# Attention with undivided probabilities, and the last batch's feed-forward spread over a recurrence's first steps

## The reference, cut to what matters

```python
# layer 0, x: (8, 256, 512)
xn = rms_norm(x, g_norm) * (1 + scale) + shift          # scale, shift from cond @ W_emb
q, k, v = heads(xn @ W_qkv)                             # 16 heads of 32
attn = softmax(rms_norm(q, g_q) @ rms_norm(k, g_k).T * 32 ** -0.5)
o = attn @ v;  x1 = o + o @ W_out
w_up, w_down = dequant4bit(...)                         # plus low-rank terms
x = x + relu(x1 @ w_up + ... + b_up) @ w_down + ... + b_down    # hidden 2048
# layer 1: a recurrence over all 256 positions
for t in range(256):                                    # q, p: (8, 512)
    q, p = rk4(q, p, drive=x[:, t])                     # four times tanh(q) @ coupling.T
    y[:, t] = q
x = x + shared_expert(y) + top2_of_8_experts(y)
```

## Time and profile before

| what | value |
| --- | --- |
| median of three runs | 3059.54 us (3057.57 to 3059.79) |
| profiled execution | 3062.81 us, of which the instructions span 3061.1 us |
| PE busy in the span | 2788.1 us (91%) |
| DVE, ACT, POOL busy | 1827.7, 1121.8, 1354.7 us |
| mean granted clock of PE | 0.921 |
| layer 0, to the barrier | 0 to 993.6 us of the span |
| the recurrence's first group, 32 steps | 1003.7 to 1219.8 us |
| the later groups, to the end | 1219.8 to 3061.1 us |

### The profile page before, as it was taken

The page is one execution under the profiler, slowest core; times in us unless marked ns, Lnnn a source line. Parts: engine busy times, 40 slices in busy tenths (PEclk is TensorE's granted clock), DMA queues, the critical chain, the costliest instruction groups (busy, mean ns, idle before and its releaser), DMA issues.

```text
span 3061.1 us, 132271 instructions
## 1 busy us (share of the span) xinstructions
PE 2788.1 (91%) x48208; PEld 2427.2 (79%) x48208; DVE 1827.7 (60%) x6585; ACT 1121.8 (37%) x4950; POOL 1354.7 (44%) x3466
## 2 busy tenths in 40 slices
PE   6778989889888556999999999999999999999998
PEld 4346667667767455999999899899899899899987
DVE  2657656755764444666666666666666666566654
ACT  1224433644552223333333333333333333333321
POOL 1220000111110666666666566566566566666600
PEclk7569999999999555999999999999999999999999
DMA  4523222533441000344444444444444344344466
GB/s 142 171 80 107 82 86 58 176 125 114 141 147 32 25 0 0 112 126 131 131 130 129 123 129 131 125 129 128 124 130 128 121 131 130 109 145 127 132 217 198
DMA packets 137163, 359.87 MB, mean 118 GB/s; under 512 B 15888, under 2 KB 24720, under 8 KB 136592
## 3 DMA queue, kind: packets, MB, share of 16 engines
q1 hardware_dynamic: 136336, 354.17, 37.8%
q10 hardware_dynamic: 672, 3.67, 0.3%
HBM read 323.31 MB, written 34.47 MB: 117 GB/s over the span
## 4 chain that ended last, share of the span: by engine, by line
PE 61%; DVE 2%; issue 2%; ACT 1%; DVEq 0%; DMA 0%; POOL 0%; POOLq 0%; SPq 0%
PE pscan L1234 13%; PE pscan L1230 13%; PE pg L1161 11%; PE pd L1187 11%; PE pu L1161 11%; ACT th L1088 1%; DVE state L1350 1%; DVE carry L1350 0%; PE prouter L1245 0%; DMA wd<-w_split 0%; PE prouter L1253 0%; PE pd L1260 0%; DVE pscan L1336 0%; DVEq L1349 0%; DVE th L1333 0%
## 5 line engine op out<-in xcount | busy, mean ns | idle before, releaser
L1230 PEld LDWEIGHTS pscan<-th,carry 128*128 128x128 f16 x16384 | 555.7, 97 | 135.6 <-ACT th L1088 114.9
L1230 PE MATMUL pscan<-th,carry 128*128 128x8 f16 x16384 | 564.4, 167 | 100.6 <-ACT th L1088 100.4
L1234 PE MATMUL pscan<-th,carry 128*128 128x16 f16 x16384 | 561.9, 170 | 3.0 <-DVE th L1333 2.3
L1234 PEld LDWEIGHTS pscan<-th,carry 128*128 128x128 f16 x16384 | 486.8, 97 | 4.5 <-DVE th L1333 4.5
L1088 ACT ACTIVATE th<-state 128x32 f16<-128x32 f32 x768 | 176.1, 229 | 733.0 <-DVE state L1350 733.0
L1161 PE MATMUL pg<-qh,wgu 128*128 128x256 f16 x3168 | 430.1, 275 | 14.5 <-issue 14.5
L1187 PE MATMUL pd<-hg,wd 128*128 128x256 f16 x3168 | 428.9, 274 | 2.8 <-DMA wd<-w_split 2.8
L1161 PE MATMUL pu<-qh,wgu 128*128 128x256 f16 x3168 | 429.2, 275 | 1.9 <-issue 1.8
L1350 DVE TENSOR_REDUCE state<-pscan 128x32 f32<-128x96 f32 x768 | 197.1, 257 | 268.0 <-PE pscan L1234 262.8
L1161 PEld LDWEIGHTS pg<-qh,wgu 128*128 128x128 f16 x3168 | 295.5, 98 | 53.3 <-issue 15.9
L1161 PEld LDWEIGHTS pu<-qh,wgu 128*128 128x128 f16 x3168 | 295.0, 98 | 37.1 <-issue 2.6
(11 more groups left out here) (203 smaller groups left out, 4573.3 us busy)
## 6 DMA issues: line engine op xcount, KB each, us to landing
wgu<-w_split SPq DMA_DIRECT2D x264, 512.0 KB, 3.6
wd<-w_split SPq DMA_DIRECT2D x264, 384.0 KB, 3.1
parts_mem<-in_w_tiles SPq DMA_DIRECT2D x120, 256.0 KB, 3.0
w_split<-parts_mem SPq DMA_DIRECT2D x99, 256.0 KB, 2.2
late<-in_w_tiles SPq DMA_DIRECT2D x78, 256.0 KB, 3.2
w_split<-late SPq DMA_DIRECT2D x33, 128.0 KB, 3.0
out<-oo SPq DMA_DIRECT2D x8, 512.0 KB, 4.0
xs<-in_x SPq DMA_DIRECT2D x1, 3584.0 KB, 13.2
```

Of the source, the lines that this page charges most:

```text
L1230: mm(pscan[:, 0, m * B:(m + 1) * B], clo[:, k, m * P:(m + 1) * P], th[:, k, 0, :], start=(m == 0 and k == 0), stop=False, skip_group_check ...
L1234: ins = mm(pscan[:, 0:2, m * B:(m + 1) * B], chi[:, k, m * P:(m + 1) * P], th[:, k], start=False, stop=(k == NC - 1), skip_group_check=True)
```

## The change

- **Probabilities stay undivided.** `normed` goes. PE transposes a head as soon as ACT has its exponential (`a_exp`). DVE takes the reciprocals of four heads at once (`inverse`), ahead of the quad's last copy. Ahead of each quad's `weighted`, PE writes the reciprocals, spread over 32 partitions each, into the free half of the same bank: eight fp32 matmuls of 128 columns with a broadcast column of `rinv` as weights and the identity as moving data. ACT copies these to `oT` (`widened`), and DVE multiplies the product by them (`gathered`).
- **The next batch's input moves forward.** ACT squares it after the first quad (was the third), PE's `norm_sum` stands in the second quad behind head 5 (was the fourth), ACT's `norm` after the second quad, DVE's `normed_input` after the third quad (was between the last two copies). PE writes these sums into the other bank's half.
- **Batch 0's pieces.** ACT converts piece 4c+4 after head 4c+2, and pieces 4c+5 to 4c+7 after head 4c+3.
- **The last batch's feed-forward is cut in two.** In layer 0 only columns 0 to 31 are made: 192 up-matmuls of 32 columns into two banks, ReLU and split in halves, 192 down-matmuls, one addition. Columns 32 to 255 are made inside the recurrence's first 32 steps: `fill` issues five matmuls of 224 columns behind each stage's `chi` product in stages 0 to 38 (up) and 41 to 79 (down), with ACT's and DVE's parts a few stages behind and POOL waiting for the result in step 31.
- **The coupling's maximum moves forward.** DVE takes it between batch 7's last `gathered` and its sums, POOL reduces it before batch 7's largest value, and `chi` is made between `scale` and `low` of batch 7.
- **The first 32 steps are written out** on all four engines: `walk`'s first loop is now one of Python. `w_up`, `w_dn`, `hid`, `late`, `fs` and `bsc` live through both layers, `w_qkv` only in layer 0, and `kp` moves from `carry` to `fs`.

```diff
+                if b == B - 1:
+                    pl.wait_ge(S["mx"], 1)
+                    pl.partition_all_reduce(kp[:, 1:2], kp[:, 0:1], P, bass.bass_isa.ReduceOp.max).then_inc(S["par"], 1)
...
-            pl.partition_all_reduce(kp[:, 1:2], kp[:, 0:1], P, bass.bass_isa.ReduceOp.max).then_inc(S["par"], 1)
...
-                    if not ffn and 3 <= h and h + 1 < PIECES:
-                        weights_high(h + 1)
                     highs(NC + h)
-                def gathered(c):
+                def pieces(h, count):
+                    for piece in range(h + NC, min(h + NC + count, PIECES)):
+                        if not ffn:
+                            weights_high(piece)
+                def widened(c):
                     act.wait_ge(S["p_pv"], b * NC + c + 1)
-                    if c == 2 and b + 1 < B:
-                        act.wait_ge(S["p_nrm"], b + 2)
-                    act.activation(oT[:, c, :], Ob[c % 2][:, 0:T], ACT.Copy).then_inc(S["a_oT"], 1)
+                    act.activation(oT[:, c, :], Ob[c % 2][:, T:2 * T], ACT.Copy).then_inc(S["a_wide"], 1)
                 for c in range(NC):
                     exps(HPC * c)
                     exps(HPC * c + 1)
                     if c:
-                        gathered(c - 1)
-                    if c == NC - 1 and b + 1 < B:
-                        norm(b + 1)
+                        widened(c - 1)
                     relus(ffn_quad[c][0:2])
                     exps(HPC * c + 2)
+                    pieces(HPC * c, 1)
                     relus(ffn_quad[c][2:3])
                     exps(HPC * c + 3)
+                    pieces(HPC * c + 1, HPC - 1)
                     relus(ffn_quad[c][3:])
-                    if c == NC - 2 and b + 1 < B:
+                    if c == 0 and b + 1 < B:
                         if b == 0:
                             act.wait_ge(S["xs_in"], 16)
                         squares(b + 1)
-                gathered(NC - 1)
+                    if c == 1 and b + 1 < B:
+                        norm(b + 1)
+                widened(NC - 1)
...
-            for j in range(RELUS):
-                relu(B - 1, j)
+            for half in range(2):
+                act.wait_ge(S["p_up"], (B - 1) * RELUS + half + 1)
+                bank = first_up[half][:, 0:RELUS * G]
+                for m in range(RELUS):
+                    part = bank[:, m * G:(m + 1) * G]
+                    ins = act.activation(part, part, ACT.Relu, bias=bsc[:, half * RELUS + m:half * RELUS + m + 1])
...
+                act.activation(hid[:, half * RELUS:(half + 1) * RELUS, 0, 0:G], bank.rearrange("p (a t) -> p a t", t=G), ACT.Copy).then_inc(S["a_up"], 1)
...
-                    pe.wait_ge(S["d_pn"], b * HEADS + h + 1)
+                    pe.wait_ge(S["a_exp"], b * HEADS + h + 1)
...
+                    if c == 1 and more:
+                        pe.wait_ge(S["a_rstd"], b + 2)
                     if c >= 2:
-                        pe.wait_ge(S["a_oT"], b * NC + c - 1)
+                        pe.wait_ge(S["d_oT"], b * NC + c - 1)
+                    pe.wait_ge(S["d_rinv"], b * NC + c + 1)
+                    for qc in range(2):
+                        for j in range(HPC):
+                            mm(Ob[c % 2][DH * j:DH * (j + 1), T + qc * P:T + (qc + 1) * P], rinv[:, HPC * c + j, qc:qc + 1].to_broadcast([P, DH]), ident[:],
+                               start=True, stop=True)
...
-                    if c == NC - 1 and more:
-                        norm_sum(b + 1)
...
+                        if (c, j) == (1, 1) and more:
+                            norm_sum(b + 1)
...
-            for part in range(2 * HC):
-                ffn_part(B - 1, part)
+            pe.wait_ge(S["d_x1"], B)
+            pe.wait_ge(S["d_x2"], 2 * (B - 1) + 2)
+            for m in range(HC):
+                for k in range(NC):
+                    for w, q in ((0, 0), (0, 1), (1, 0)):
+                        ins = mm(first_up[m // RELUS][:, m % RELUS * G:(m % RELUS + 1) * G], w_up[:, k, w, m * P:(m + 1) * P], x1s[:, k, q, 0:G],
+                                 start=(k == 0 and w == q), stop=(k == NC - 1 and w == 1))
+                if m % RELUS == RELUS - 1:
+                    ins.then_inc(S["p_up"], 1)
+            for m in range(NC):
+                for k in range(HC):
+                    if m == 0 and k % RELUS == 0:
+                        pe.wait_ge(S["d_up"], (B - 1) * RELUS + k // RELUS + 1)
+                    for w, q in ((0, 0), (0, 1), (1, 0)):
+                        ins = mm(D[1][:, m * G:(m + 1) * G], w_dn[:, k, w, m * P:(m + 1) * P], hid[:, k, q, 0:G],
+                                 start=(k == 0 and w == q), stop=(k == HC - 1 and w == 1))
+            ins.then_inc(S["p_dn"], 1)
...
-                def normed(h):
...
+                def inverse(c):
+                    dve.wait_ge(S["a_exp"], b * HEADS + HPC * (c + 1))
+                    dve.reciprocal(rinv[:, HPC * c:HPC * (c + 1), :], psum_e[:, HPC * c:HPC * (c + 1), :]).then_inc(S["d_rinv"], 1)
+                def gathered(c):
+                    dve.wait_ge(S["a_wide"], b * NC + c + 1)
+                    dve.tensor_tensor(oT[:, c, :], Ob[c % 2][:, 0:T], oT[:, c, :], ALU.mult).then_inc(S["d_oT"], 1)
...
                     row_max(h + 1)
-                    normed(h)
                     row_max(h + 2)
-                    normed(h + 1)
+                    if c:
+                        gathered(c - 1)
                     turned(h)
                     lows(b, ffn_quad[c][0:2])
                     row_max(h + 3)
-                    normed(h + 2)
                     turned(h + 1)
                     lows(b, ffn_quad[c][2:3])
-                    normed(h + 3)
                     turned(h + 2)
-                    if c == NC - 1 and b + 1 < B:
-                        normed_input(b + 1)
+                    inverse(c)
                     turned(h + 3)
                     lows(b, ffn_quad[c][3:])
+                    if c == 2 and b + 1 < B:
+                        normed_input(b + 1)
                     if ffn and c == NC - 1:
                         second(b - 1, 0)
+                gathered(NC - 1)
+                if b == B - 1:
+                    dve.wait_ge(S["coupling_in"], 16)
+                    dve.tensor_reduce(kp[:, 0:1], coupling, AX.XY, ALU.max, apply_absolute_value=True).then_inc(S["mx"], 1)
...
+                if b == B - 1:
+                    dve.wait_ge(S["par"], 1)
+                    tie(dve.tensor_scalar(kp[:, 1:2], kp[:, 1:2], 2.0 ** -60, None, ALU.max))
...
-            dve.wait_ge(S["coupling_in"], 16)
...
-            dve.wait_ge(S["d_x1"], B)
-            dve.tensor_reduce(kp[:, 0:1], coupling, AX.XY, ALU.max, apply_absolute_value=True).then_inc(S["mx"], 1)
-            due(1)
-            dve.wait_ge(S["par"], 1)
-            tie(dve.tensor_scalar(kp[:, 1:2], kp[:, 1:2], 2.0 ** -60, None, ALU.max))
...
+            tie(dve.tensor_scalar(Z["chi"], coupling, kp[:, 3:4], None, ALU.mult))
+            low(B - 1)
+            tie(dve.scalar_tensor_tensor(Z["clo"], coupling, kp[:, 3:4], Z["chi"], ALU.mult, ALU.subtract))
...
+            def first_low(half):
+                dve.wait_ge(S["a_up"], (B - 1) * RELUS + half + 1)
+                h = hid[:, half * RELUS:(half + 1) * RELUS, :, 0:G]
+                dve.tensor_tensor(h[:, :, 1, :], first_up[half][:, 0:RELUS * G].rearrange("p (a t) -> p a t", t=G), h[:, :, 0, :], ALU.subtract).then_inc(S["d_up"], 1)
+            first_low(0)
+            first_low(1)
...
-            due(RELUS - last_low[0])
-            for i in range(2):
-                second(B - 1, i)
+            dve.wait_ge(S["p_dn"], 2 * (B - 1) + 1)
+            dve.wait_ge(S["x_biased"], B)
+            slots = xv[:, :, B - 1, 0:G]
+            dve.scalar_tensor_tensor(slots, D[1][:, 0:NC * G].rearrange("p (c t) -> p c t", c=NC), kd[(B - 1) % 2], slots, ALU.mult, ALU.add)
...
+        FILL, PAUSE = 5, 3
+        def fill_stage(n):
+            return n // FILL + (PAUSE if n >= NC * HC * 3 else 0)
+        def pair_stage(j):
+            return fill_stage(24 * j + 23)
+        def half_stage(i):
+            return fill_stage(NC * HC * 3 + 96 * i + 95)
         def walk(eng, step, last_tile):
-            with eng.Fori(0, G // 2) as i:
+            for i in range(G // 2):
...
+                if not tile and t == G - 1:
+                    pl.wait_ge(S["f_out"], NC)
...
+                    if not tile:
+                        for j in range(HC // 2):
+                            if pair_stage(j) + 1 == 4 * t + s:
+                                fill_relu(j)
+                            if pair_stage(j) + 2 == 4 * t + s:
+                                fill_high(j)
...
+            def fill_relu(j):
+                act.wait_ge(S["f_up"], j + 1)
+                for i in range(2):
+                    half = bank_up[j % 2][:, i * (T - G):(i + 1) * (T - G)]
```

(41 more changed lines are left out.)

100 lines of the change are left out of this document (46 added, 54 removed).

## The result

The changed kernel takes **2987.22 us** (median of four runs, 2984.80 to 2989.23) against 3059.66 of the kernel before beside it: ratio 0.9764, 95% interval 0.9747 to 0.9781, or 72 us less.

A forecast was written before the change was run, and what follows sets the result against it. Batch 0 is bound by handovers, batches 1 to 7 by PE with holes, the first group by a chain of short steps. Terms -32.4 + 9 - 5 - 21 = -49.4 gave 3010 us, range 2990 to 3028.

The forecast's parts named there:

- Part 1: Last batch's feed-forward: 45.9 us shrinks to 12.5 + 1.0, so -32.4 us, with small matmuls at 27 ns.
- Part 2: Seam between the layers: 0 us, POOL's unexplained wait behind the barrier kept whole.
- Part 3: Fill inside the recurrence's first group: +9 us, 78 stages each 0.11 us longer at 1.2 GHz.
- Part 5: Batch 0: -21 us from earlier weight pieces and removed scalings (-8 to -24).
- The term for the restores: Batch 0, weight restores: pieces staged earlier, -5.8 us in quads 1 and 2 each, -3.2 in quad 0.
- Part 4: Attention in batches 1 to 7: net -4.5, taken as -5 us (+10 to -13).
- 23.1 us recovered on PE: Batches 1 to 7: removed reciprocals and scalings and the earlier input step shorten PE's waits by 23.1 us.
- 28 spreads at 0.6: Batches 1 to 7: the added spreads of reciprocals on PE cost 16.8 us (14 to 31).
- a stall of 0.3 in six batches: DVE making the next input before the last quad's maxima: estimated +0.3 us in each of six batches, 1.8.
- the clock's rival: First group: the clock rises during the fill, -4 for +9 us, total 2997 us; chance 0.28.
- The attention giving its gain back: Rival: loads or lora pace batch 0 (-8), a spread costs 1.0 us, total 3034 us; chance 0.16.
- The refills of the written-out code: Rival, first group: some 39 instruction refills stop the chain 2.5 us each, +97 us, 3107 us; chance 0.04.

The follow-up runs named there:

- e6: Changed kernel with eight instead of five fill matmuls in a stage of the first group: 2975.85 us.
- h10: Changed kernel with eight fill matmuls a stage and eight matmuls of unread result in every other first-group stage: 2970.98 us.
- h12: Changed kernel with eight fills, other stages kept full, GpSimd touched early, weight pieces shared out anew, input step at its old place in batch 0 alone: 2953.01 us.
- h9: Changed kernel with the second layer's weight pieces shared out anew in batches 4 to 7 (3, 3, 3, 2 in the projections' steps): 2976.45 us.
- e3: Kernel before with 14 idle matmuls ahead of the first head's transposes and 14 ahead of the last weighted product, batches 1 to 7: 3055.26 us.
- e8: Changed kernel with DVE's preparation of the next batch's input back at its old place in the last quad: 2992.02 us.

## Why the forecast was right and where it was wrong

- **Part 1, the tail (-32.4): right**, -32.8. One of its terms lies in the row above, ahead of `low`: the +1.0 for DVE's added steps, of which PE's wait before the first up-product shows 0.7 (6.18 to 6.87 us). The choice of 27 ns a matmul, against 109 from the other bound, was the one that mattered, and 192 in 5.2 us bear it out. The coupling's load and its all-reduce were in time.
- **Part 2, the seam (0): right**, -0.4, and keeping a wait that I could not explain was right too. What it hangs on is now known, an all-reduce before it, and that it could be had: 7 us. I could have read it in the trace of before.
- **Part 3, the fill (+9): right in sign and near in size**, +7.0. The clock stayed at 1.2 GHz as taken, but one of the two reasons given for it is not enough: the hole before the group is there with eight fills a stage as well (e6, h10), and the clock rises all the same. A stage is 1.79 instead of 1.81 us, since five fills issue in 0.88 and not 0.93. The pause before the down-products costs one stage of 2.30 us, 0.6 more than its neighbours, where up to 1 us was allowed and not added. The rule of the Trainium skill (TensorE: Matmul & The Clock Gate, The HAM clock gate), that sustained activity releases the throttle, was weighed against the row and set aside. The runs show both: five fills a stage left PE without a gap for two stretches of 39 stages and the clock stayed low; eight a stage brought it up 3 to 7 us behind the group's first sum (4.5 in e6, 7.2 in h10, 3.4 in h12). The rule holds for the denser stage, and a PE without gaps in the profile is not by itself enough.
- **Part 5, batch 0 (-21): right**, -21.2 from the input's product. The term for the restores (5.8 in quads 1 and 2 each) measured 6.4 and 5.0; taking the new places of the pieces back costs 14.1. That the sum agrees to 0.2 us is in part luck: quad 0 gave 1.2 us for 3.2, the last quad and what follows it 7.7 for 6.6, the projections 1.0 that the sum did not have, and one trace of the same batch 0 (h10) is 3.7 us shorter. It missed that the input step ahead of the last maxima costs about 1 us here.
- **Part 4, batches 1 to 7 (-5): the step that failed**, by 18 us. Its first term, 23.1 us recovered on PE, is right (25.0; at the last weighted products 15.2 for 13.2, at the transposes 10.7). Its second, 28 spreads at 0.6, is too high: 0.46 each by the trace and by the doubled spreads, 12.9 for 16.8, 4 us. Its third, a stall of 0.3 in six batches, did not come: 2 us. The fourth was the large one: the short stretches at 1.2 GHz were left at zero in the sum and put into the low end of the range alone. They fell from 38 to 19 us (16 to 19 in the seven like traces), worth half of that difference, and 9.5 us of shorter busy time are seen in four groups of PE's instructions. The trace of before had announced it: each of its eight low stretches in batches 1 to 7 begins inside the wait before the first transpose or the last weighted product, or at most 1.1 us behind it, and the forecast removed the waits and kept the stretches. h9 and e3 show the link: waits taken out or filled, the low stretches behind them are gone.
- **The sum.** -32.4 + 9 - 5 - 21 = -49.4 stands against -32.8 + 7.0 - 23.2 - 21.2 = -70.2, and -0.4, -5.4 and +2.5 from the seam and from the scatter of an execution. The range did not hold what it claimed: with every part at its own low end (-34, -4, -13, -24) the sum is -75, or 2985 us, below the 2990 that was to cover the forecast and the clock's rival with their bounds.
- **The rivals.** The clock rising during the fill did not happen at five a stage, and does at eight. The attention giving its gain back is the opposite of what came. The refills of the written-out code cost nothing that the time shows.

The remaining 1.6 us of batches 1 to 7 (-21.6 explained, -23.2 seen) cannot be told from the scatter of a trace. What stays open is what separates five fills a stage from eight for the clock; no run was made at six or seven.

## What to carry to other kernels

Price a removed wait of TensorE at its own length and then ask what the clock did behind it: where the profile has low-clock stretches after the waits, a wait of some 4 us cost up to twice its length here (h9), one of 1.5 us little more than itself (e8). A step that is moved has to be priced in every place where it lands; the one that saved 1.8 us a batch in six batches cost about 1 in the first. Before a term is read off a single trace, look at the same stretch in the other traces that leave it unchanged: here it differed by 3 us in batches 1 to 7 and by 5 in batch 0. In a stage that a chain of small steps bounds, fill up to what fits at the low clock (four here) or enough to bring the clock up (eight), since the amount in between (five) was the worst of the three.

## What the hardware did that I had not expected

- After a partition_all_reduce, GpSimd's next tensor operation began 7.2 us later (some 8 us behind the barrier where it came after that), the touched one as the drive product, without anything in the trace that it waits for, while memset and affine_select went through at once. One 128x1 operation put behind the last all-reduce takes the wait off the path. The Trainium skill (GPSIMD Engine Reference, Instruction dispatch) has about 6 us for the first call of a freshly loaded kernel, with no instruction of its own in the profile. The trace agrees in kind, with a somewhat longer wait (6.9 to 7.2 us in the trace of before), but places it before the first standard operation behind the all-reduce: the all-reduces of batches 0 to 7 themselves begin 0.1 us behind the DVE operation that they wait for.
- A fuller stage can be a shorter one: eight matmuls of 224 columns more made a stage 1.64 us, where it was 1.70 without any.
- Doubling 28 spreads at 0.46 us cost 9 us where 12.8 were added, against the changed kernel's own trace: the clock was low for 8 us instead of 19. Against the other traces it is 10 to 12.
